# A graph network on one core: the read-back of all queries for the first attention pass is issued later in SyncE's program

## What is computed

```python
k = _typed_matmul(h, k_linears, node_type).reshape(n, N_HEADS, D_K)
q = _typed_matmul(h, q_linears, node_type).reshape(n, N_HEADS, D_K)
v = _typed_matmul(h, v_linears, node_type).reshape(n, N_HEADS, D_K)
q_att = jnp.einsum('nhd,rhde->rnhe', q, relation_att)
v_msg = jnp.einsum('nhd,rhde->rnhe', v, relation_msg)
...
score = jnp.sum(q_att[etype, col_idx] * k[row_idx], axis=-1) * (relation_pri[etype] / SQRT_DK)
...
alpha = ex / denom[col_idx]
agg = segment_sum(alpha[..., None] * v_msg[etype, row_idx], col_idx)
```

## Time and profile before

| | |
|---|---|
| median of 3 runs | 3327.05 us (3326.5 to 3329.18) |
| profiled execution, its own time | 3328.74 us |
| its span in the trace | 3326.9 us |
| busy share of the span: PE, DVE, POOL, ACT | 84%, 75%, 65%, 58% |
| Projections, last stage copy ends | 1333.7 us into the span |
| first attention pass: first gather, last fetch on PE | 1347.8 us, 1882 us |

### The profile page before, as it was taken

The page is one execution under the profiler, slowest core; times in us unless marked ns, Lnnn a source line. Parts: engine busy times, 40 slices in busy tenths (PEclk is TensorE's granted clock), DMA queues, the critical chain, the costliest instruction groups (busy, mean ns, idle before and its releaser), DMA issues. The chain is left out here.

```text
span 3326.9 us, 57628 instructions
## 1 busy us (share of the span) xinstructions
PE 2806.1 (84%) x14883; PEld 1774.0 (53%) x14883; DVE 2497.6 (75%) x6123; ACT 1940.3 (58%) x6302; POOL 2166.5 (65%) x2298
## 2 busy tenths in 40 slices
PE   5799899999989799588888775899998896888776
PEld 5666555555556455355555553666666653333332
DVE  8899889999977555599999843899998874444444
ACT  1478745555542354389999821788888753333334
POOL 4777677777767542677777465777776314777775
PEclk9999989999999899799999988899999997566675
DMA  6234488888871588888777656777777444333335
GB/s 198 90 98 126 119 267 261 264 262 264 264 191 40 153 323 347 288 259 245 245 235 236 174 167 198 234 237 236 232 229 224 111 203 166 106 105 106 105 106 118
DMA packets 260608, 651.27 MB, mean 196 GB/s; under 512 B 66797, under 2 KB 115642, under 8 KB 253514
## 3 DMA queue, kind: packets, MB, share of 16 engines
q0 software_dynamic: 141840, 474.50, 46.9%
q1 hardware_dynamic: 118458, 173.08, 16.0%
HBM read 505.42 MB, written 145.27 MB: 196 GB/s over the span
## 5 line engine op out<-in xcount | busy, mean ns | idle before, releaser
L2155 POOL DMA_INDIRECT a_rows<-table,met x568 | 541.4, 953 | 206.8 <-issue 153.2
L3753 PE MATMUL ps<-rows_in,hot_w 128*128 128x256 f32 x832 | 424.0, 619 | 111.9 <-ACT hot_w L3721 71.7
L1354 POOL DMA_INDIRECT rows_in<-table,met x416 | 411.7, 990 | 143.9 <-issue 104.5
L3695 POOL DMA_INDIRECT rows_in<-table,met x416 | 393.4, 946 | 143.8 <-issue 119.4
L3799 DVE TENSOR_TENSOR xs<-xs,ps 128x256 f32 x416 | 175.1, 421 | 282.5 <-PE ps L3753 277.6
L3753 PEld LDWEIGHTS ps<-rows_in,hot_w 128*128 128x128 f32 x832 | 188.9, 278 | 347.0 <-ACT hot_w L3721 212.1
L3721 ACT ACTIVATE hot_w<-hot,met 128x128 f32<-128x128 f32 x416 | 166.6, 401 | 354.3 <-PE ps L3753 339.9
L2637 PE MATMUL ps<-a_rows,a_hot 128*128 128x260 f32 x1136 | 315.6, 405 | 20.9 <-DVE acc L2643 17.8
L2643 DVE TENSOR_TENSOR acc<-acc,ps 128x520 f32 x416 | 286.1, 688 | 38.0 <-PE ps L2637 29.8
L2155 POOL DMA_INDIRECT xs<-table,met x264 | 253.3, 960 | 93.0 <-issue 71.0
L857 POOL DMA_INDIRECT records<-rec,rows x241 | 258.0, 1071 | 84.7 <-issue 72.3
(11 more groups left out here) (488 smaller groups left out, 6279.7 us busy)
## 6 DMA issues: line engine op xcount, KB each, us to landing
a_hot_t<-one_hots SPq DMA_DIRECT2D x104, 256.0 KB, 5.4
table<-stage SPq DMA_DIRECT2D x25, 1024.0 KB, 3.8
rows_in<-table,met POOLq DMA_INDIRECT x832, 3.7
one_hots<-hot_t SPq DMA_DIRECT2D x52, 256.0 KB
dst_row<-slot_rows SPq DMA_DIRECT2D x51, 256.0 KB, 5.0
by_dst<-dst_rows SPq DMA_DIRECT2D x25, 512.0 KB, 5.7
by_dst<-lo_rows SPq DMA_DIRECT2D x24, 512.0 KB, 4.2
a_rows<-table,met POOLq DMA_INDIRECT x568, 3.9
```

The costliest lines, as they stand in the source:

```text
L1354: e.indirect_dma_start(self.rows[:, n % self.RING, 0:2 * D], None, self.table, bass.IndirectOffsetOnAxis(ap=self.b.met[:, n, R_SRC:R_SRC + ...
L2155: e.indirect_dma_start(self.row(n, 0, self.width), None, self.table, bass.IndirectOffsetOnAxis(ap=b.met[:, n, self.word:self.word + 1], ax ...
L3695: e.indirect_dma_start(self.rows[:, n % self.RING, :], None, self.table, bass.IndirectOffsetOnAxis(ap=self.b.met[:, n, R_REL:R_REL + 1], a ...
L3753: e.matmul(b.ps[:, n % self.BANKS, 0:D], self.hot_w[:, n % GRP_H, :], self.rows[:, n % self.RING, :], start=True, stop=True).then_inc(self ...
```

## The change

SP waits for two more things before it issues the read-back: the landing of the table's puts of the tiles 25 and 26, that is of the last puts but one. The transfer itself, its size and its queue stay as they are, and all other engines keep their programs.

```diff
         e.wait_ge(self.seg.kept, 5)
         for t in range(NS - self.QS, NS):
             e.wait_ge(*self.q_stored(t))
+        for t in range(NS - self.SLOTS, NS - 1):
+            e.wait_ge(*self.stored(t))
         e.dma_start(self.q_parts[:, :, :], self.q_rows[0:NP, :].rearrange("(t p) f -> p t f", p=P)).then_inc(self.q_back.sem, 16)
         self.finished(e)
```

## The result

The changed kernel took 3340.75 us (median of 14 runs, 3333.27 to 3350.32) against 3330.84 us for the kernel before in the same sessions: a ratio of 1.0028, 95% interval 1.0019 to 1.0037. It is slower by 6 to 12 us. The ratio is of the fast runs alone: two of the 14 runs before took 4268 and 5190 us, and the median without them is 3329.9. Forecast were 3330.0 us, with 3323 to 3336 for the likeliest case and the faster rival, and a chance of 0.18 for slower by over 0.2%. Some 3 us of the distance between 3340.75 and 3330.0 are the kernel before itself, which in these sessions took more than the 3327.05 us that the forecast started from.

A forecast was written before the change was run, and what follows sets the result against it. Window 0's start, held by the last put and late gathers, was taken to set the kernel's end one for one. Median 3327.05 + 1.9 (10.0 late less 8.1 of waits) + 1 for ScalarE = 3330.0 us, range 3323 to 3336.

The forecast's parts named there:

- likeliest case: Whole kernel: the read-back gets 0.22 MB/us beside gathers, giving 3330.0 us, own range 3326 to 3336; chance 0.64.
- faster rival: Start of window 0: gathers take little from the read-back (0.33 MB/us), the last put's 4.0 us are won, 3323 us; chance 0.14.
- can have landed any time before: End of Projections: the read-back's landing is hidden behind the last put's at 1347.04, so the read-back is covered.
- Steps 1 and 2: End of Projections: read-back issued at 1335.0, 38 us later; last put lands in 8.6 us, 4.0 us earlier.
- get ahead of the last put: Rival at the last put: nothing starts earlier, first product 7 us late, total 3327 to 3330 us; chance 0.08.
- Step 3: Read-back before window 0: 3.5 MB left beside the gathers at 0.22 MB/us take 15.9 us, landing at about 1361.7.
- The bound of 0.165: Slow bound of the read-back's rate beside gathers, in MB/us: it would land at 1367.
- The rival of turns packet by packet: Beside the gathers: one-for-one packets leave the read-back 0.11 MB/us, +19.4 us, 3346 us, +0.6%; chance 0.10.
- Step 4: Start of window 0: one-hots queue 1.5 us behind the read-back; first fetch 1363.2, VectorE's first product 1365.0, 10.0 us later.
- Steps 5 and 6: Window 0: three gather waits, 8.1 us, go, adds 1.9 us later; the path through `below` gives 2 us, plus 1 for ScalarE.
- ScalarE's lead: Window 0: ScalarE no longer weighs chunks in advance while VectorE waits for gathers; 1 us added for it.
- The clock's rival: Adds of window 0: TensorE still at the low clock, half a window adds 7 us, 3337 us; chance 0.04.

The follow-up runs named there:

- e3_gathers_wait: The changed kernel with POOL waiting for the read-back ahead of its first gather; ratio to the kernel before 1.0028 (1.0016 to 1.0039).
- e6_behind_hots_warm: e5_behind_hots plus 80 matmuls nobody reads on TensorE ahead of its wait for the read-back; ratio to the kernel before 0.9980 (0.9971 to 0.9990).
- e4_split: The changed kernel with tiles 0 to 4 read back at the old place, only tiles 5 to 24 late, awaited at chunk 32; ratio to before 1.0006.
- e7: The changed kernel plus 220 matmuls nobody reads on TensorE in its wait for the read-back; ratio to the kernel before 1.0061 (1.0046 to 1.0077).
- e8: The changed kernel with the read-back waiting for the last put too (tiles 25 to 27); ratio to the kernel before 1.0033 (1.0021 to 1.0045).
- e9: The changed kernel plus 140 matmuls nobody reads on TensorE in its wait for the read-back; ratio to the kernel before 1.0013 (1.0004 to 1.0022).
- e5_behind_hots: e4_split with the second transfer (tiles 5 to 24) issued behind the pass's first masks and one-hots on SP; ratio to before 0.9988 (0.9979 to 0.9997).
- e2_halves: The changed kernel with tiles 13 to 24 read back at the old place, only tiles 0 to 12 late, TensorE awaiting both; ratio to before 0.9990.
- e10_behind_hots_warm40: e5_behind_hots plus 40 matmuls nobody reads on TensorE ahead of its wait for the read-back; ratio to the kernel before 0.9989 (0.9980 to 0.9998).
- e1: The changed kernel with the read-back waiting for puts of tiles 22 to 24 instead of 25 and 26; ratio to before 1.0012 (1.0002 to 1.0021).

## Why the prediction was wrong

**What bounds the kernel, and where the change acts: right, with less room than I wrote.** The last put alone stood on the path, and the read-back was covered, but not with time to spare. Between 1302 and 1344 us the DMA engines were full in the kernel before (share 1.01), and the read-back had what the puts left, 4.72 MB in 42 us or 0.11 MB/us. Its last packets moved between 1346.0 and 1346.6 (queue q1 in 1346:1347), about 0.5 us ahead of the last put's landing at 1347.04:

```profile
q1 hardware_dynamic: 21, 0.03, 7.1%
```

So "can have landed any time before" was too wide, and the 31% to spare, read before the read-back began, were all used. A shift at the start of the pass went through to its end one for one in this pair (7.8 us at the fourth window, 7.6 at the last). It isn't a rule: in e3_gathers_wait and e6_behind_hots_warm later windows at a lower clock changed the shift by 4 to 6 us.

**Steps 1 and 2: right.** Issue at +1.0 (forecast +0.6), last put landed in 8.6 us (8.6), first gather at +9.4 (+9.4). The read-back didn't get ahead of the last put.

**Step 3, the read-back's own time: this is the step that failed, by its rate, and the larger part of the miss.** I took 0.22 MB/us beside gathers and got a landing at +27.3; it was 0.17 MB/us and +30.7. The row that I chose, 1350:1356, shows SP's queue while the gathers were behind with what they had been asked for, at 0.12 MB/us. Beside a transfer that had run for some time they took 0.21 MB/us, all that POOL issues, and the read-back had what was left of the 0.38. I had written down the gathers' demand of 0.21 in step 5 and didn't use it here. The total wasn't at hand: the 0.34 that I worked with would have left 0.13 and a landing near +38, 7 us too late where I was 3.4 too early. The amount moved ahead of the gathers was sized well at first (1.5 MB by +11.4, as forecast), and then the read-back had the engines for itself 2 us longer, since the gathers' data came some 4 us behind POOL's first issue and not 2. The bound of 0.165 held; as the value it would have given a landing at +32.6. The rival of turns packet by packet can't be judged by 1540 packets to 906. At 0.38 in all, one for one would offer the gathers 3.3 KB of each 4.8, 0.26 MB/us, and they ask for 0.21; so such turns would leave the read-back the same 0.17. The rival's 0.11 came from a total of 0.34 and from giving the gathers more than POOL issues. What speaks against turns is only the start in the kernel before, 1022 packets to 216, and what holds the gathers back there is open.

**Step 4, the one-hots: right in kind.** From the landing to the first fetch 2.1 us, forecast 1.5; with the 1.6 us to the first product (1.46 forecast, and 1363.2 + 1.46 are 1364.7, not the 1365.0 that I wrote) it stands at +34.4 where I had +30.6, 3.8 us off, 3.4 of them from step 3. e4_split shows that the queueing was real, and larger than its price here: with TensorE free of the read-back it costs 17 us.

**Steps 5 and 6, what is given back: too high by 1.1 us, and for another reason than named.** The waits for gathers went, all three; the gathers moved 0.21 MB/us beside the read-back where I had 0.12, so they were there sooner than I needed. From the first product to the adds VectorE took 28.65 us instead of 35.62, 7.0 less where I had 8.1. TensorE's fetches set the pace at two places now. This is VectorE's wait for them in 1365:1395 (total, times, longest); the longest, 2.8 us, is the one ahead of the first product, and the other 1.2 us are the 1.1 that are missing:

```profile
DVE a_prod L2486 <- PE ps L2472: 4.0, 3, 2.8
```

Behind the adds window 0 took 21.9 us, and the window before 21.0; the 0.9 us is what I had put in for ScalarE's lead. It isn't ScalarE: in e4, e7, e8 and e9 it has as much to do in this window (19.3 to 19.6 us, in the changed kernel 19.75, before 17.07), and they run it in 20.4 us at 1.00. It is 1.5 us that go with the clock of 0.95 (VectorE waits 1.2 us for TensorE's fetches in it), less the 0.5 us for gathers that the window before had.

The sum, at the fourth add window: forecast 10.0 - 8.1 + 1 = 2.9 us, measured 13.8 - 7.0 + 0.9 and rounding = 7.8. Of the 4.9 us between them 3.8 are the first product's place and 1.1 the giving back. With 7.8 us the 6.65 us of 0.2% are passed, and 3327 + 7.8 = 3335 would have been inside the range. The whole kernel is 9.3 us slower by its ratio (6 to 12), of which the pass in the profile holds 7.6; 1.1 us more lies behind it in the profile, which is within what that part scatters by.

**The chances.** My likeliest case had its end at a rate of 0.165, and I gave 0.05 to it being slower by over 0.2%; the measured rate of 0.17 lay near that end. There is a slip as well. The recorded text puts the rate at which 0.2% is passed at 0.17, but its own steps give 7.7 us at 0.17 (landing 1366.4, one-hots 1368.3, product 1369.8, so 14.8 - 8.1 + 1) and 6.65 only near 0.18. So the rates between 0.17 and 0.18 were counted as harmless and aren't. The demand was in the rows, so this isn't bad luck.

**The rivals.** The faster rival was half right: the last put's 4.0 us were there, and e5_behind_hots takes them and 2 more, but only without the wait for the whole read-back. The clock's rival happened in a small form, 1 to 2 us instead of 7.

## What to carry to other kernels

A transfer is covered by the room that it finds while it runs, and one that ends just in time has none left: look where its last packets move before calling it covered. Moving its issue behind the last busy stretch puts most of its duration onto the path (here 29.7 us, of which 16.5 showed at the first fetch), and what it gives back is only what it had slowed on the path (here one put, 4 us against 14). To price a transfer beside another stream, take the total that the engines move with packets of these sizes and subtract what the other stream asks for in its steady state; a short stretch in which that stream is only starting shows a share that won't last. And look for how much of the transfer the first work needs: five of 25 tiles early, the rest behind the small loads that the next stage waits for, made the same kernel faster than either version, by 1 to 7 us against before.

## What the runs showed of the hardware

- SP's issue of a small mask took 8.31 us in the changed kernel and 14.73 us in e8_behind_last, where it stands behind the 3200-packet read-back, against 0.56 us before. It took 4.85 in e3_gathers_wait and 2.16 behind the 3.9 MB of e4_split, but 0.55 behind the 2.56 MB of e2_halves: the issuing instruction itself is held while much is left in the queue ahead of it. I saw no cost of it beyond the one-hots' delay; no run takes the two apart.
- A window of adds takes 20.4 us at a granted clock of 1.00 (e4, e7, e8 and e9 in window 0), and 21.0 to 23.3 where the clock is lower, without one length for one clock: 21.0 at 0.97 (e5), 21.9 and 22.5 at 0.95, 21.5 and 22.3 at 0.92, 22.3 and 23.3 at 0.90. Which it gets differs between kernels with the same work ahead of the adds, and 1.00 during the wait before didn't secure it (e10_behind_hots_warm40: 0.90).
- The DMA engines move 0.38 MB/us in all, whether the read-back is alone (3.75 MB in 10 us, e3_gathers_wait) or shares them with gathers (5.34 MB in 14 us). Beside the puts with their packets of 16 KB it was more (405 GB/s in 1302:1344 of the kernel before).
- The last put, 2 MB, lands in 7.1 us with nothing beside it (e8_behind_last), in 8.3 to 8.6 with a transfer issued about 1 us behind it (changed, e2, e4), and in 12.2 to 12.6 beside one that is already running (e1, before).
- The first gathers behind a restart are late even where no HBM-to-HBM copy stands in SP's first batch: in e5_behind_hots VectorE's second product waits 3.37 us for them, as the 3.33 before. What in the masks, the one-hots and, there, the read-back holds them back is open.
